# Attention's weights folded behind the first expert stage, a first routing in groups of 2, 2, 4, 4 and 4 tiles, and adds of one expert in flight together

## The reference

```
x = x + 0.5 * experts(layernorm(x))
x = x + attention(layernorm(x))
x = x + 0.5 * experts(layernorm(x))

experts: logits = x @ gate (256 x 8); the top 2 of 8, softmax over the two
         out = sum over the two of weight * (silu(x @ w0[e]) * (x @ w1[e])) @ wout[e]   (256 -> 512 -> 256)
attention (16 heads, 64 + 64 wide):
         q = rms_norm(x @ wq_a) * q_norm @ wq_b     (64 latents -> 16 x (64 plain + 64 rotated))
         c = x @ wkv_a                              (64 latents + 64 rotated, shared by all heads)
         k, v = rms_norm(c) * kv_norm @ wkv_b       (16 x (64 + 64))
         out = softmax(q k^T / sqrt(128)) v @ wo
```

## Time and profile before

| | |
|---|---|
| median of three runs | 1098.09 us (1097.34, 1098.09, 1104.69) |
| the profiled execution | 1111.73 us, its span 1109.5 us |
| PE, PE weight loads | 92%, 73% of the span busy |
| DVE, ACT, POOL | 65%, 47%, 43% |
| granted TensorE clock, mean | 0.986 |
| first routing, to the first expert matmul | 0 to 90.1 us |
| first expert stage, to the landing of its last add | to 293.3 us |
| turn to attention, to the first scores | to 318.9 us |
| attention and second routing | to 900.6 us |
| second expert stage | to the end |

### The profile page before, as it was taken

One profiled execution on the slowest core, in us unless ns is written; L12 is line 12 of the kernel. 1 busy time (PEld: TensorE's weight loads), 2 busy tenths in 40 slices (PEclk: granted clock), 3 DMA queues, 4 the chain that ended last, 5 costly groups with the idle time before them and its releaser, 6 DMA issues.

```text
span 1109.5 us, 22666 instructions
## 1 busy us (share of the span) xinstructions
PE 1022.8 (92%) x6232; PEld 808.0 (73%) x6233; DVE 726.3 (65%) x1649; ACT 524.6 (47%) x1139; POOL 473.3 (43%) x417
## 2 busy tenths in 40 slices
PE   4548999999879999999999999999999879999995
PEld 4436888888557777777777777777688648888884
DVE  6344566664377778878887788777546746656542
ACT  1224343332156677676767677666501313533321
POOL 2541343443344454646355654443225513344432
PEclk9999999999998999999999999999999989999998
DMA  9833455433200110111111011111476545644330
GB/s 241 274 111 96 106 140 125 109 51 49 63 1 10 58 39 26 33 40 39 39 39 30 30 39 39 39 39 39 154 227 210 185 134 110 163 107 104 53 57 8
DMA packets 71615, 95.87 MB, mean 86 GB/s; under 512 B 9616, under 2 KB 48656, under 8 KB 71312
## 3 DMA queue, kind: packets, MB, share of 16 engines
q1 hardware_dynamic: 56656, 77.51, 22.8%
q0 software_dynamic: 14304, 16.87, 9.1%
q10 hardware_dynamic: 576, 0.53, 0.2%
HBM read 64.37 MB, written 34.43 MB: 89 GB/s over the span
## 4 chain that ended last, share of the span: by engine, by line
PE 53%; DMA 26%; issue 9%; DVE 7%; POOLq 1%; ACT 1%; another core or an unknown queue 1%; POOL 1%; SPq 0%; DVEq 0%; ACTq 0%
DMA x_after_moe<-shared,small 13%; DMA out<-shared,small 12%; PE bank L1720 11%; PE bank L1747 10%; PE bank L1708 5%; PE bank L1709 5%; PE bank L1710 5%; PE bank L1819 3%; PE bank L1695 2%; PE bank L1696 2%; PE bank L1521 1%; PE bank L1523 1%; PE bank L1525 1%; PE bank L1662 1%
## 5 line engine op out<-in xcount | busy, mean ns | idle before, releaser
L874 ACT ACTIVATE shared<-bank,small 128x512 f32<-128x512 f32 x256 | 176.7, 690 | 93.0 <-DVE small L1334 92.1
L1334 DVE TENSOR_REDUCE small<-bank 128x1 f32<-128x512 f32 x256 | 174.9, 686 | 43.7 <-PE bank L1710 43.4
L1720 PE MATMUL bank<-constants,shared 128*128 128x128 f32 x1024 | 157.0, 276 | 2.1 <-ACT shared L883 1.1
L810 ACT CAST split_rows_and_inner<-bank 128x512 fp32r<-128x512 f32 x78 | 45.8, 588 | 238.5 <-PE bank L1506 199.4
L1720 PEld LDWEIGHTS bank<-constants,shared 128*128 128x128 f32 x1024 | 123.1, 141 | 44.7 <-issue 14.3
L1523 PE MATMUL bank<-expert_weights_low,split_rows_and_inner 128*128 x312 | 144.2, 462 | 0.0
L1525 PE MATMUL bank<-expert_weights_high,split_rows_and_inner 128*128 x312 | 143.1, 459 | 0.0
L1521 PE MATMUL bank<-expert_weights_high,split_rows_and_inner 128*128 x312 | 125.2, 401 | 3.5 <-DVE split_rows_and_inner L1119 3.4
L1708 PE MATMUL bank<-expert_weights_high,shared_split 128*128 128x512 f32 x256 | 123.5, 483 | 3.7 <-DVE shared_split L1402 2.3
L1124 DVE TENSOR_TENSOR split_rows_and_inner<-bank,split_rows_and_inner 128x512 fp32r<-128x512 f32 x78 | 53.9, 691 | 106.1 <-ACT split_rows_and_inner L810 104.4
L573 POOL DMA_INDIRECT x_after_moe<-shared,small x39 | 61.2, 1569 | 143.2 <-DMA x_after_moe<-shared,small 90.2
(11 more groups left out here) (197 smaller groups left out, 2192.7 us busy)
## 6 DMA issues: line engine op xcount, KB each, us to landing
expert_weights<-L_ffn_w_kernel SPq DMA_DIRECT2D x32, 512.0 KB
shared<-rows_by_expert SPq DMA_DIRECT2D x78, 129.0 KB
expert_weights<-L_ffn_wo_kernel SPq DMA_DIRECT2D x16, 512.0 KB
shared<-inverse_sums SPq DMA_DIRECT2D x64, 128.0 KB, 3.0
attended_transposed<-shared SPq DMA_DIRECT2D x32, 256.0 KB, 3.1
expert_weights<-attended_transposed SPq DMA_DIRECT2D x2, 2048.0 KB, 10.1
shared<-attended_transposed SPq DMA_DIRECT2D x2, 2048.0 KB
rows_by_expert<-empty_rows SPq DMA_DIRECT2D x19, 129.0 KB
```

Of the source, the lines that this page charges most:

```text
L874: nc.scalar.activation(prob[k % 4], bank[k % 4][:, :], ACT.Exp, bias=negmax[:, k % 8:k % 8 + 1], accum_out=psum[par][:, hh * GT + qt:hh * ...
L1334: V.tensor_reduce(negmax[:, k % 8:k % 8 + 1], bank[k % 4][:, :], AX.X, ALU.max, negate=True).then_inc(max_ready, 1)
L1720: last = tr(bank[4 + k % 2][:, c * P:(c + 1) * P], prob[k % 4][:, c * P:(c + 1) * P], ident)
```

## The change

- The 16 tiles of the first routing are worked in five groups of 2, 2, 4, 4 and 4 tiles (`GROUPS[0]`). Their normed rows lie in one buffer for all 16 tiles (`rows0`), so no group waits for another's stores, and their slots are kept apart. The statistics, roots and norms are placed anew between the groups; POOL now issues the stores of a group after the root of the group two further on.
- SP loads the constants in two parts: first only what the routing needs, then the first two tiles of x, the token ids and the gate; the rest of x follows. The rope tables, the projection weights and wo are loaded behind the first two experts. The head weights come from the host already turned per head, and are loaded at tile 3 of the first expert stage; the transposes of the fold are gone.
- Of the eight stores of zero rows in the first routing ACT issues four.
- PE runs 6 dummy products of 384 columns before the first expert stage.
- The fold stands behind the first expert stage: DVE scales the key weights and makes the rope weights, PE makes the 32 query products after 2 dummies and before 8 more; the 16 value products are behind the first projection, in the place of 5 dummies, in banks 7, 0, 1 and 7. The scaling by norm weights has moved into the copies of ACT and DVE. POOL makes the first pair's weights after the first two roots, and waits for the value products before it keeps the values.
- In both expert stages the add of tile t waits for the landing of the add of tile t - 2, and for that of t - 1 only if t is the first tile of its expert (a table `land_tab`, read by POOL before each add).

```diff
-GN = (GT, 2)
+GROUPS = (((0, 2), (2, 2), (4, GT), (8, GT), (12, GT)), tuple((2 * g, 2) for g in range(NT // 2)))
+GN = 2
...
+VALUE_BANKS = (7, 0, 1, 7)
...
+        o = 2 * GT * D + 3 * ROW + 2 + 2 * MLP + 3 * D
+        o += -o % 4
+        rows0 = area(o, [NT, TOPK, ROW])
+        rope_w = area(o, [PAIRS, 2, ROPE])
+        qnT, knT, vT = (area(o + (k + 1) * NH * HD, [NH, HD], HD) for k in range(3))
+        stage_o = area(o + NT * TOPK * ROW, [NH, D], HD)
...
-            sp.dma_start(cst[:, :], const).then_inc(const_in, 16)
+            first = x_in[0].rearrange("(t p) d -> p t d", p=P)
+            sp.dma_start(cst[:, 0:C_KCOS], const[:, 0:C_KCOS]).then_inc(const_in, 16)
+            sp.dma_start(xall[:, 0:GN, :], first[:, 0:GN, :]).then_inc(x_in_sem[0], 16)
             sp.dma_start(ids[:, :], ids_in).then_inc(const_in, 16)
             sp.dma_start(gate_sb[:, :, :], gate.rearrange("(c p) e -> p c e", p=P)).then_inc(const_in, 16)
-            for g in range(NG):
+            sp.dma_start(xall[:, GN:GT, :], first[:, GN:GT, :]).then_inc(x_rest_in, 16)
+            for g in range(1, NG):
                 sp.dma_start(xall[:, g * GT:(g + 1) * GT, :],
                              x_in[g].rearrange("(t p) d -> p t d", p=P)).then_inc(x_in_sem[g], 16)
-            sp.dma_start(wproj[:, :, 0:2 * HD], wkv_a.rearrange("(c p) n -> p c n", p=P)).then_inc(attw_in, 16)
-            sp.dma_start(wproj[:, :, 2 * HD:3 * HD], wq_a.rearrange("(c p) n -> p c n", p=P)).then_inc(attw_in, 16)
-            sp.dma_start(norm_w[0:HD, 1:2], kvn_w.rearrange("(p a) -> p a", a=1)).then_inc(attw_in, 16)
-            for k in range(2):
-                sp.dma_start(norm_w[k * HD:(k + 1) * HD, 0:1], qn_w.rearrange("(p a) -> p a", a=1)).then_inc(attw_in, 16)
-                sp.dma_start(stage_q[k * HD:(k + 1) * HD], wq_b).then_inc(attw_in, 16)
-            sp.dma_start(stage_kv, wkv_b).then_inc(attw_in, 16)
-            sp.dma_start(stage_o, wo.rearrange("(h v) n -> v h n", v=HD)).then_inc(attw_in, 16)
+
+            def load_tables():
+
+                sp.dma_start(cst[:, C_KCOS:C_ALL], const[:, C_KCOS:C_ALL]).then_inc(attw_in, 16)
+                sp.dma_start(wproj[:, :, 0:2 * HD], wkv_a.rearrange("(c p) n -> p c n", p=P)).then_inc(attw_in, 16)
+                sp.dma_start(wproj[:, :, 2 * HD:3 * HD], wq_a.rearrange("(c p) n -> p c n", p=P)).then_inc(attw_in, 16)
+                for k in range(2):
+                    rows_ = slice(k * HD, (k + 1) * HD)
+                    sp.dma_start(norm_w[rows_, 0:1], qn_w.rearrange("(p a) -> p a", a=1)).then_inc(attw_in, 16)
+                    sp.dma_start(norm_w[rows_, 1:2], kvn_w.rearrange("(p a) -> p a", a=1)).then_inc(attw_in, 16)
+                sp.dma_start(kvn_row[:, :], kvn_w.rearrange("(a n) -> a n", a=1).to_broadcast([HD, HD])).then_inc(attw_in, 16)
+
+            def load_head_weights():
+
+                for k in range(2):
+                    sp.dma_start(rope_w[k * HD:(k + 1) * HD].rearrange("p a h n -> p (a h n)"), wq_rope).then_inc(attw_in, 16)
+                for to, w in ((qnT, wq_in), (knT, wk_in), (vT, wv_in)):
+                    sp.dma_start(to.rearrange("p h n -> p (h n)"), w).then_inc(attw_in, 16)
+
+            def load_output_weights():
+
+                sp.dma_start(stage_o, wo.rearrange("(h v) n -> v h n", v=HD)).then_inc(attw_in, 16)
...
+            load_tables()
+            load_output_weights()
...
-                for e in range(E // 2 if f else E):
+                for e in range(E // 2):
...
+                    if f == 0 and among(t, 3):
+                        load_head_weights()
...
+                    if t > 3:
+                        landed = pool.value_load(land_tab[0:1, t:t + 1], min_val=16, max_val=16 * (TILES // 3))
...
                     pool.wait_ge(y_sb[f], t + 1)
-                    if t > 0:
+                    if t > 1:
+                        pool.wait_ge(added[f][(v - 2) % 3], (t - 2) // 3 * 16 + 16)
+                    if t > 3:
+                        pool.wait_ge(added[f][(v - 1) % 3], landed)
+                    elif t > 0:
                         pool.wait_ge(added[f][(v - 1) % 3], (t - 1) // 3 * 16 + 16)
-                    pool.sem_inc(add_due[f], 1)
+                    pool.sem_inc(pool_issue, 1)
...
-            for g in range(NG):
+            for g, (t, n) in enumerate(GROUPS[0]):
                 pool.wait_ge(veps_ready[0], g + 1)
-                root(0, g * GT, GT)
-            for g in range(NG):
+                root(0, t, n)
+                if g >= 2:
+                    scatter(0, g - 2)
+            for g in range(len(GROUPS[0]) - 2, len(GROUPS[0])):
                 scatter(0, g)
             pool.wait_ge(xd_copied, 16)
...
+            pool.wait_ge(attw_in, 16 * 14)
+            root_first(0)
+            root_first(1)
             pool.wait_ge(folded_w, 2)
             pool.wait_ge(wa_ready, 1)
             load_weights(0, 0)
-            root_first(0)
-            root_first(1)
             root_rows(1)
             root_latents(0)
+            pool.wait_ge(fold_psum, 6)
             keep_values(0)
...
+            act.wait_ge(tables_ready[0], 1)
+            for e in range(E // 2, E):
+                n = act.value_load(cnt_i[0:1, e:e + 1], min_val=0, max_val=T)
+                nc.scalar.dma_start(xs[bass.ds(n + e * REGION, P), :], zrow[:, :]).then_inc(tails_zeroed[0], 16)
...
+            for e in range(2):
+                for piece in range(3):
+                    split_high(0, e, piece)
...
+            act.wait_ge(attw_in, 16 * 14)
+            act.wait_ge(scaled_w, 1)
+            for k in range(2):
+
+                act.wait_ge(fold_psum, k + 1)
+                src = bank[4 + k][:, :].rearrange("p (a h n) -> p a h n", a=4, h=2)
+                for hh in range(2):
+                    last = nc.scalar.activation(wpair[:, 4 * k:4 * k + 4, 2, (1 - hh) * HD:(2 - hh) * HD], src[:, :, hh, :],
+                                                ACT.Copy, scale=norm_w[:, 0:1])
+                last.then_inc(folded_w, 1)
+
+            def value_weights(k, b):
+
+                act.wait_ge(fold_psum, 2 + k + 1)
+                nc.scalar.activation(wvo[:, 2 * k:2 * k + 2, :].rearrange("p a n -> p (a n)"), bank[b][:, :],
+                                     ACT.Copy, scale=norm_w[:, 1:2]).then_inc(folded_v, 1)
+
             rows_out(0, 0, 0)
             for half in range(2):
                 latents_out(0, half, 2 + half)
             squares(0)
+            for k, b in enumerate(VALUE_BANKS):
+                value_weights(k, b)
...
+                own.step(V.tensor_scalar(alone, tfirst, 0.0, 16.0, ALU.is_equal, ALU.mult))
+                own.settle()
+                own.step(V.tensor_tensor(land_tab, alone, cst[:, C_LAND:C_LAND + TILES], ALU.add))
...
+            def first_stats(g):
+                t, n = GROUPS[0][g]
+                dve.wait_ge(x_rest_in if g == 1 else x_in_sem[t // GT], 16)
+                ln_stats(xall[:, t:t + n, :], t, n, veps_ready[0])
+
+            def norm_first(g):
+                t, n = GROUPS[0][g]
+                dve.wait_ge(rstd_ready[0], g + 1)
+                ln_rows(0, g, xall[:, t:t + n, :], t)
+
+            groups = len(GROUPS[0])
             own.step(V.memset(zero8, 0.0))
+            first_stats(0)
             dve.wait_ge(const_in, 48)
             own.step(V.tensor_copy(rank_ops[:, 0:2 * P], cst[:, C_UP:C_UP + 2 * P]))
             own.step(V.tensor_scalar(carry, iota_e, 0.0, None, ALU.mult))
-            def first_stats(g):
-                dve.wait_ge(x_in_sem[g], 16)
-                ln_stats(xall[:, g * GT:(g + 1) * GT, :], g * GT, GT, veps_ready[0])
-
-            def norm_first(g):
-                dve.wait_ge(rstd_ready[0], g + 1)
-                norm_rows(0, g, xall[:, g * GT:(g + 1) * GT, :])
-
-            first_stats(0)
+            norm_first(0)
             first_stats(1)
-            norm_first(0)
+            xt_out(0, 0, xTr[0])
+            norm_first(1)
             first_stats(2)
-            xt_out(0, 0, xTr[0])
-            for g in range(NG):
-                if g + 1 < NG:
+            for g in range(groups):
+                if 0 < g < groups - 1:
                     norm_first(g + 1)
-                if g == 0:
-                    first_stats(3)
                 choose(0, g)
-                if g + 1 < NG:
+                if g + 1 < groups:
                     xt_out(0, g + 1, xTr[0])
+                if g + 3 < groups:
+                    first_stats(g + 3)
                 find_slots(0, g)
             tables(0)
-
-            dve.wait_ge(scattered[0][2], 16 * GT * TOPK)
-            dve.wait_ge(scaled_w, 2)
-            q_rope_w = stage_q.rearrange("p (a h n) -> p a h n", a=PAIRS, h=2)
+            moe(0)
+
+            dve.wait_ge(attw_in, 16 * 14)
+            own.step(V.tensor_scalar(norm_w[:, 0:1], norm_w[:, 0:1], SCALE, None, ALU.mult))
+            own.settle()
```

(47 more changed lines are left out.)

191 lines of the change are left out of this document (85 added, 106 removed).

## The result

The changed kernel takes **1088.1 us** (median of four, 1087.05 to 1089.77) against 1100.9 for the kernel before on the same chip (median of four): ratio 0.988, interval 0.984 to 0.991. On two other chips it took 1086.1 and 1087.7 against 1095.5 and 1096.9: 0.991 (0.989 to 0.993) and 0.992 (0.989 to 0.995). The profiled execution took 1089.1, its span is 1087.3. 1089 was forecast. Several of the reasons on record were wrong all the same; the experiments sort them out.

What follows compares the result with a forecast made beforehand. TensorE was taken to bound all but the first routing, the turn to attention, the second routing and the tail of adds. From the median 1098.09 us, -9.2 (start) + 2.0 (turn) - 1.6 (last tail) = -8.8 gave 1089 us, range 1079 to 1096.

Steps and rivals of the forecast that it cites:

- The start: First routing, up to the first expert matmul: 17.5 us sooner in the profile, 9.2 of it from the change.
- undisturbed start: First routing of the kernel before without the profiled stop: first expert matmul at 81.8 instead of 90.10 us.
- The stop in every run: Rival, first routing: ScalarE's 12.14 us wait on an unknown releaser is in every run; median loses 17.1, 1081 us; chance 0.25.
- POOL is not slowed: Rival, first routing: VectorE's subtractions do not slow POOL's stores; last store 61.1, 3.9 us more gain, 1085 us; chance 0.17.
- The turn: From experts to attention: value products of 7.0 us replace 4.46 us of dummies and delay the key transposes, +2.0 us.
- So the gain of the first tail is lost: 0: Turn to attention: adds land 2.2 us earlier, but the fold and dummies hold TensorE until 299.6; gain 0.
- On average keep up ... Overlapping them can win these tails and nothing per tile.: Expert stages: serial adds keep pace with the tiles, so overlapping gains only behind each stage's last result.
- The term on record: Last tail, end of the second expert stage: last add issued 0.9 us after its result, -1.6 us.
- The per-tile time: Expert stages: stays at TensorE's pace, 4.88 us a tile.
- Slower, two adds in flight land later: Rival, expert stages: overlapped adds share 16 DMA engines and land later; 1113 us at 5.2 us an add; chance 0.06.
- The head weights' loads: nothing: First expert stage, tile 3: five more loads (1.3 MB), about 3 us in SyncE's queue, cost nothing.
- The sum: Whole kernel against the median: start -9.2, turn +2.0, last tail -1.6, in all -8.8 us, giving 1089 us.

Runs made afterwards that it cites:

- A second profile: The kernel before, unchanged, run and profiled once more: median 1097.0 us, ratio 0.999 to its other runs.
- the old layout: Layout of the kernel before; its three profiles are two of that kernel unchanged and one with only its adds overlapped (1091.1 us against 1096.9).

## Why the prediction was right, and where it was not

The time and the range held. Step by step:

- **The start.** First store 17.5 (18.1 forecast); gap gone; three stores slowed by 1.0 us each, 3.0 in all (3.9 forecast, six by 0.65); last store 63.2 (65.0); first expert matmul 70.6 (72.6). As a difference against an undisturbed start: -8.4 us (-9.2).
- **The stop in every run** fell. A second profile had none, nor had that of overlapping adds alone.
- **POOL is not slowed** fell: it was, by 3.0 us. That agrees with the Trainium skill, GPSIMD Engine Reference, "Key points": a VectorE instruction with two SBUF inputs contends with POOL.
- **The turn**, +2.0: +2.2 in the profile (the mean of three profiles after less that of two before is 1.5), by another cause: this agreement is luck. The mis-sized term is the 16 value products, 3.67 us for 7.0. I took their duration from a stretch at the lower rate, and that of the query products too (2.08 for 3.68). The granted clock and the last add's landing made the difference instead. "So the gain of the first tail is lost: 0" came out for another reason as well: the fold holds nobody, but the last add, issued 2.2 us sooner behind its result, takes about 2 us longer to the reload, which comes 6.1 us behind the result for 6.4.
- **"On average keep up ... Overlapping them can win these tails and nothing per tile."** This is the step that failed. I read one last add of each stage (3.6 and 3.0 us behind its result, start to start) and took it for the tail. In three profiles with serial adds it lay anywhere from 3.0 to 7.2 us. The adds alone are worth 5.9 us in the kernel before and up to 12 in the changed one, where a part may be the clock's. The term on record is 1.6. "Nothing per tile" was nearly right: 0.8 us a stage.
- **The per-tile time**, 4.88: it was 4.87, right.
- **Slower, two adds in flight land later** fell: the median landing is 3.8 us in both kernels.
- **The head weights' loads: nothing** holds only where adds overlap. With serial adds the second add, beside these loads, was the first of the late ones (7.5 us to the next).
- **The sum.** It came out by luck: two errors cancel. The adds had 1.6 us and brought 5.9 (4.3 too little); start and turn had 9.2 - 2.0 = 7.2 and brought 3.4 (3.8 too much), though the start itself is 8.4 us sooner in the traces: the turn takes more back than forecast.

The two parts are not independent. With serial adds the moved fold and the early start together brought nothing (1099.5 against 1096.4). Why is shown in part only. Both turns begin at the reload: the first scores come 25.5 to 27.1 us behind it in the three profiles of the old layout, 26.6 to 28.6 in the three of the changed kernel and 28.3 with serial adds; where the projection ran at the lower rate it alone took 1.4 to 2.3 us more. And in the old layout a reload 2.2 us sooner brought the scores 2.1 us sooner. So the old turn hides a late last add no better than the new one. But in the profile with serial adds the row of adds falls behind sooner, beside the head weights' loads, and the last one of stage one comes 7.2 us behind its result, for 3.6 in both profiles of the kernel before.

## What to carry to other kernels

A serial chain whose period is hardly below the loop's (4.6 to 4.8 us for 4.87) is not hidden: each late item is paid back over ten rounds or more, and whatever waits for the last one gets the remainder. Look at the share of such a DMA in the chain that ended last, and at the distance from producer to consumer in the middle of the loop, not at the last pair. Take a TensorE duration from a stretch with the same rate as the one to which it moves.

## What the hardware showed unasked

- A store from POOL beside VectorE's subtraction of two SBUF operands took 1.9 to 2.0 us against 0.96; the subtractions kept their pace of 1.15 us.
- The granted clock reads 1.00 where the trace has no clock record yet. In the kernel before the records begin at 94.4 us; the 512-column matmuls from 90 to 94 follow each other at 0.43 us under a 1.00, and at 0.23 from there on. So the rate in a first stretch is read from the matmuls, and mean clocks of kernels whose records begin at different times (59 us in the changed kernel) are not compared.
- VectorE's copy of two columns (L1134, 0.16 us at the median) took 3.71 us beside POOL's subtraction of 2.98 us (L559), in the first profile of the kernel before.
- From the issue of the last add of stage one to the reload it took 2.8 us with nothing beside it (four profiles of four) and 4.3 to 5.3 beside the weights' work (nine of ten).
